# A graph kernel's first layer: gathers that wait for edge counts, and counts put ahead of a group's sums

## The chip, the cores and the metric

The kernel runs on one core of one Trainium2 chip. The metric is the device time of one execution in microseconds. Engines are named as the profile has them: PE is TensorE's matrix multiply (PEld its weight loads), DVE is VectorE, ACT is ScalarE, POOL is GpSimd, SP is SyncE.

## The reference

Four graph layers over 6,250 nodes of 128 features and 206,250 edges, each followed by a residual sum and a layer norm:

```python
x = _layernorm(x + _L0_gnn_ref(x, ..., src, dst, edge_type_8), axis=-1)   # two relational layers
x = _layernorm(x + _L1_gnn_ref(x, src, dst), axis=-1)                     # sum over neighbours
x = _layernorm(x + _L2_gnn_ref(x, edge_index, ...), axis=-1)              # attention over 12,500 slots
x = _layernorm(x + _L3_gnn_ref(x, edge_attr_128, src, dst), axis=-1)      # sum of node and edge rows
```

The first relational layer, which is where the change lies, is per node

```python
T = jnp.einsum('nd,rdf->rnf', h, W)
msg = T[etype, src] * norm
agg = jax.ops.segment_sum(msg, dst, num_segments=N)
h = relu(bn(agg + h @ self_loop[l]))
```

Edges are sorted by their target `dst`.

## The kernel before

The program runs through phases: preparation, first layer (`phase_first`), second relational layer, the neighbour sum, attention, the edge sum. The later phases work on dense matrices of edge counts (how many edges go from node a to node b), and the first layer makes these counts beside its own work.

**A tile of the first layer.** 6,250 nodes are 49 tiles of 128 targets (`NT`). The edges of a tile lie in 35 slots of 128 edges (`SLOTS`), in 7 groups of 5 (`GROUPS`, `PER`). For each group:

- SyncE waits on `ring` until the same group of the tile before is summed, then loads the edges' records (L627) and their attribute rows (L631).
- GpSimd waits for the records (`rec_in`), then issues 5 indirect DMAs, one per slot, each of which gathers 128 rows of the table of messages into `rows` (L643). When they have landed, `gathered[g]` has risen.
- VectorE makes 0/1 masks of the edges' targets (`hot`, L1024, and `rows`' last columns, L1025) and raises `hot_made`.
- TensorE waits for `gathered`, `hot_made` and `attr_in`, and adds the group into one PSUM bank by 5 matmuls, mask by rows (L756; a 4-byte matmul shows as two records, so a group is x10). The last one raises `ring`.

After group 6 VectorE takes the sum out (`take`, L948) and `close` makes the node's new row.

**The counts.** TensorE also ranks the edges of a tile by source tile (`rank_quarter` in groups 0 to 3, L662 and L665; `rank_left` in group 4, L672 and L677), VectorE turns ranks into places, and TensorE places the edges (`place`, L688, in group 0 of the next tile). For the tile t - 1, during the groups of tile t, TensorE makes the counts by small matmuls of 32 rows (`count`, L700 and L705). The 49 source tiles are 4 blocks (`BLOCKS`) of 16, 16, 16 and 1. Blocks 0 to 3 are done in groups 2 to 5, each after that group's sum and ranking. A block is 8 + 64 matmuls (8 + 4 for the last), all four quarters into the one PSUM tensor `cnt`.

**What orders the counts.** `count(t, b)` waits for VectorE's `shot` masks (`shot_made`, L1008) and for `cnt_moved`, that is until ScalarE has copied all of block b - 1 out of `cnt` (L857, four copies) into `mine`. TensorE turns the copied counts by transposes (`turn_counts`, L723): turn 0 in group 3, 1 in group 4, 2 in group 5, 3 in group 6 (`FLIP_AT`), turns 4 to 6 of the tile before that in groups 0 to 2 (`FLIP_LATER`), always as the last work of the group. ScalarE works strictly in its program's order: for block b it first does `move_turned(t, b - 1)`, which waits for turn b - 1, makes two copies (L816, L817) and issues two stores (L821), and only then waits for `counted` and copies block b out. For block 0 it is `move_turned(t - 1, 6)` that stands ahead.

`counted` starts at 2 and rises by one for each block; `ring` starts at 7. Both are counted up over all tiles. The order of each engine's work is written out by hand in the blocks of `phase_first`; no planner orders it.

Of the kernel before, what the change touches and what calls it, by code (L numbers as in the profile page):

```python
# [19 lines left out]
NT = -(-NODES // P)  # L20
# [27 lines left out]
BLOCKS = [(b * BANK, min(BANK, NT - b * BANK)) for b in range(-(-NT // BANK))]  # L48
# [474 lines left out]
    return r  # L523


def phase_first(nc, k):

    with ExitStack() as ctx:
# [3 lines left out]
        def sem(name):  # L532
            k.sems.append(nc.alloc_semaphore(name="f_" + name))
            return k.sems[-1]
# [72 lines left out]
        srow_out, shot_made, counted, cnt_moved, stored = sem("srow_out"), sem("shot_made"), sem("counted"), sem("cnt_moved"), sem("stored")  # L607
# [6 lines left out]
        @block.sync  # L614
        def _(e):
            with e.Fori(0, NT) as t:
                for u in range(QUARTERS):
                    c = e.value_load(k.wlo[0:1, bass.ds(t * QUARTERS + u, 1)], min_val=0, max_val=REAL_CHUNKS)
                    e.wait_ge(wrec_used, t)
                    e.dma_start(wrec[:, u * QCOLS:(u + 1) * QCOLS, :].rearrange("p a b -> p (a b)"),  # L620
                                k.rec_d[bass.ds(c * (CHUNK * REC), P * QCOLS * REC)].rearrange("(p c) -> p c", p=P))\
                     .then_inc(wrec_in, 16)
                c = e.value_load(k.tlo[0:1, bass.ds(t, 1)], min_val=0, max_val=REAL_CHUNKS)
                for g in range(GROUPS):
                    s = slice(g * PER, (g + 1) * PER)
                    e.wait_ge(ring, t * GROUPS + (g + 1))
                    e.dma_start(recs[:, s, :].rearrange("p a b -> p (a b)"),  # L627
                                k.rec_d[bass.ds(c * (CHUNK * REC), P * SLOTS * REC)]
                                .rearrange("(p c) -> p c", p=P)[:, g * PER * REC:(g + 1) * PER * REC])\
                     .then_inc(rec_in[g], 16)  # L630
                    e.dma_start(rows[:, s, D:2 * D],  # L631
                                k.ins["edge_attr_128"][bass.ds(c * CHUNK, P * SLOTS), :]
                                .rearrange("(p j) f -> p j f", p=P)[:, s, :]).then_inc(attr_in[g], 16)

        @block.gpsimd
        def _(e):
            with e.Fori(0, NT) as t:
                for g in range(GROUPS):
                    e.wait_ge(rec_in[g], (t + 1) * 16)
                    e.wait_ge(ring, t * GROUPS + (g + 1))  # L640
                    e.sem_inc(turn, 1)
                    for j in range(g * PER, (g + 1) * PER):
                        e.indirect_dma_start(  # L643
                            out=rows[:, j, 0:D], out_offset=None, in_=k.table_d[0],
                            in_offset=bass.IndirectOffsetOnAxis(ap=recs[:, j, 4:5].bitcast(I32), axis=0),
                        ).then_inc(gathered[g], 16)

        @block.tensor
        def _(e):
# [30 lines left out]
            def place(t, first):  # L680

                e.wait_ge(puts_made, t + 1)
                if not first:
                    e.wait_ge(by_dst_moved, t * NSEG - (NSEG - GROUPS + len(FLIP_LATER)))
                for u in range(QUARTERS):
                    for c in range(QCOLS):
                        a = u * QCOLS + c
                        m = e.matmul(pm[0:CELLS + 1, u * 3 * QW:(u + 1) * 3 * QW], put_col[:, a, :],  # L688
                                     put_row[:, a, :, :].rearrange("p x r -> p (x r)"), start=c == 0, stop=c == QCOLS - 1)
                m.then_inc(placed, 1)  # L690

            def count(t, b):

                lo, n = BLOCKS[b]
                e.wait_ge(shot_made, t * (len(BLOCKS) + 1) + (b + 2))
                e.wait_ge(cnt_moved, (t * len(BLOCKS) + b) * QUARTERS)
                for i in range(2):
                    for u in range(QUARTERS):
                        q = slice(u * QW, (u + 1) * QW)
                        e.matmul(cnt[:, u, 0:n * QW], shotx[q, i, :], xhot[q, i, lo * QW:(lo + n) * QW],  # L700
                                 start=i == 0, stop=False)
                for j in range(n):
                    for u in range(QUARTERS):
                        q = slice(u * QW, (u + 1) * QW)
                        m = e.matmul(cnt[:, u, j * QW:(j + 1) * QW], shot[q, b % 2, j, :], dhot[q, lo + j, :],  # L705
                                     start=False, stop=j == n - 1)
                m.then_inc(counted, 1)
# [18 lines left out]
            def turn_keys(t):  # L726

                e.wait_ge(key_moved, t + 1)
                for x in range(3):
                    m = e.transpose(kk[:, x, :], key_t[:, x, :], k.ident16[:, :])  # L730
                m.then_inc(key_ps, 1)
# [16 lines left out]
            def tile(t, first, second):  # L748
                for g in range(GROUPS):
                    e.wait_ge(gathered[g], (t + 1) * (16 * PER))  # L750
                    e.wait_ge(hot_made, t * GROUPS + (g + 1))
                    e.wait_ge(attr_in[g], (t + 1) * 16)
                    if g == 0:
                        e.wait_ge(acc_free, t)
                    for j in range(g * PER, (g + 1) * PER):
                        m = e.matmul(acc[:, 0:GW], hot[:, j, :], rows[:, j, :], start=j == 0, stop=j == SLOTS - 1)  # L756
                    m.then_inc(ring, 1)
                    if g == 0 and not first:
                        place(t - 1, second)
                    if g < QUARTERS:  # L760
                        rank_quarter(t, g)
                    if g == QUARTERS:
                        rank_left(t)
                    if not first:
                        if g == 0:
                            turn_keys(t - 1)
                        if g == 1:
                            turn_h(t - 1, second)
                        if g == 2:
                            self_terms(t - 1, second)  # L770
                        if 2 <= g < 2 + len(BLOCKS):
                            count(t - 1, g - 2)
                        if g in FLIP_AT:
                            turn_counts(t - 1, FLIP_AT[g])
                        elif not second:
                            turn_counts(t - 2, FLIP_LATER[g])
# [1524 lines left out]
```

## Time and profile before

| | us |
|---|---|
| median of 3 runs | 6612.25 |
| lowest, highest | 6593.21, 6656.78 |
| profiled execution, own time | 6709.38 |
| its span | 6707.6 |

The profile is that of one execution. Its page gives busy times and shares of each engine, waits with their releasers (an arrow `<-` names who ended the wait; "issue" is a wait for nothing that the profile shows; "remote" one whose releaser it cannot name), and the timeline gives single instructions in order of time, merged where they follow each other. A row of the windows view has the stretch, its length, then busy us and instructions of PE, PEld, DVE, ACT and POOL, the granted clock of TensorE, the DMA engines' busy share and GB/s. The DMA queue q0 is GpSimd's. In a timeline row the first number is the start and the second the length, both in us.

### The profile page before, as it was taken

The numbers are of one execution on the slowest core, as the hardware profiler recorded it, in microseconds if no ns is written. First come the engines' busy times: TensorE is split into PE (matmuls) and PEld (weight loads), VectorE is DVE, ScalarE is ACT, GpSimd is POOL, SyncE is SP. The second block draws the span as 40 slices with busy tenths as digits, with TensorE's granted clock in tenths as the row PEclk, the third lists the DMA queues.
The fourth block names the chain that finished last, engine by engine and source line by source line (L and its number), as shares of the span: only waits on it lengthen the run. The fifth ranks groups of instructions, "written<-read, shape, count | busy, mean of one in ns | idle before, by whom it ended". The sixth has DMA issues, their size and how long they took to land. (4 is left out here: it accounts for less than half of the span.)

```text
span 6707.6 us, 157901 instructions
## 1 busy us (share of the span) xinstructions
PE 4545.6 (68%) x54120; PEld 3396.8 (51%) x54121; DVE 3830.7 (57%) x8330; ACT 2425.1 (36%) x3822; POOL 2436.6 (36%) x2046
## 2 busy tenths in 40 slices
PE   5465655656555555555655499999989466666778
PEld 2244444444444444444444366666645266666767
DVE  4155555554455544545545566666630689999843
ACT  2123333233233223223223366666610145555600
POOL 0444544444444444444444000000000067777700
PEclk8677777777777777777777699999989778888889
DMA  5444444444444444444444422222258234444378
GB/s 201 132 123 138 146 142 136 134 138 138 134 135 137 133 127 137 134 129 142 138 128 146 137 77 77 80 77 76 80 193 284 74 148 153 153 153 153 105 249 259
DMA packets 673171, 935.65 MB, mean 139 GB/s; under 512 B 150771, under 2 KB 567006, under 8 KB 666174
## 3 DMA queue, kind: packets, MB, share of 16 engines
q1 hardware_dynamic: 470114, 548.86, 25.7%
q10 hardware_dynamic: 146524, 270.11, 10.9%
q0 software_dynamic: 56448, 115.72, 6.9%
q8 instruction: 32, 0.52, 0.0%
q14 instruction: 53, 0.43, 0.0%
HBM read 653.23 MB, written 281.17 MB: 139 GB/s over the span
## 5 line engine op out<-in xcount | busy, mean ns | idle before, releaser
L643 POOL DMA_INDIRECT f_rows<-table,f_recs x1715 | 1652.8, 964 | 1960.1 <-DMA f_recs<-edge_records 1162.4
L756 PE MATMUL f_acc<-f_rows,f_hot 128*128 128x264 f32 x3430 | 1181.9, 509 | 368.3 <-issue 295.4
L756 PEld LDWEIGHTS f_acc<-f_rows,f_hot 128*128 128x128 f32 x3430 | 848.5, 257 | 567.2 <-issue 351.9
L2013 PE MATMUL a_psum<-state_and_spare,a_weights 128*128 (+1 forms) x4802 | 662.4, 308 | 296.9 <-DVE a_weights L2131 152.4
L1963 POOL TENSOR_TENSOR a_weights<-a_powers,a_counts 128x896 f32<-128x896 f16 x245 | 719.6, 2945 | 336.9 <-ACT a_powers L2053 305.9
L2013 PEld LDWEIGHTS a_psum<-state_and_spare,a_weights 128*128 128x128 f32 x4802 | 651.6, 224 | 310.6 <-issue 203.8
L1224 ACT ACTIVATE g_grow<-g_gps 128x512 f16<-128x512 f32 x1225 | 667.1, 595 | 343.1 <-PE g_gps L1161 342.6
L816 ACT ACTIVATE f_counts_by_destination<-f_pm 128x896 f16<-128x896 f16 x343 | 314.7, 917 | 1085.3 <-PE f_pm L723 864.2
L705 PE MATMUL f_cnt<-f_dhot,state_and_spare 32*128 32x32 f16 x9604 | 238.4, 182 | 643.2 <-issue 642.7
L1181 PE MATMUL g_zps<-g_ohot,g_grow 32*128 32x256 f16 x19992 | 655.3, 269 | 0.7 <-issue 0.6
L1263 DVE TENSOR_SCALAR g_ohot<-count,slot_target 128x256 f16<-128x256 f16 x2499 | 537.1, 281 | 153.1 <-PE g_zps L1181 147.8
L1008 DVE TENSOR_TENSOR state_and_spare<-f_count_up,f_key 128x2048 f16<-128x2048 f16 x196 | 349.6, 1784 | 419.8 <-PE f_cnt L705 347.7
L897 DVE TENSOR_TENSOR f_put_row<-f_sort,f_by_cell 128x490 f16<-128x490 f32 x196 | 130.4, 665 | 740.1 <-PE f_sort L665 413.8
L705 PEld LDWEIGHTS f_cnt<-f_dhot,state_and_spare 32*128 32x128 f16 x9604 | 170.1, 95 | 746.3 <-issue 715.8
L1181 PEld LDWEIGHTS g_zps<-g_ohot,g_grow 32*128 32x128 f16 x19992 | 457.9, 93 | 158.5 <-issue 119.4
L1145 POOL DMA_INDIRECT g_grow<-high_low_rows,g_lcur x49 | 46.4, 946 | 1142.1 <-PE g_zps L1181 1142.1
L2117 DVE SCALAR_TENSOR_TENSOR a_powers<-a_psum,a_leaky_from,a_diag 128x896 f32 (+1 forms) x343 | 379.0, 1141 | 59.7 <-POOL a_weights L1963 37.7
L857 ACT ACTIVATE state_and_spare<-f_cnt 128x512 f16<-128x512 f32 (+1 forms) x784 | 326.4, 502 | 225.7 <-issue 223.9
L1161 PE MATMUL g_gps<-g_hl,g_shot 128*128 128x256 f16 (+1 forms) x2450 | 378.2, 275 | 35.1 <-DVE g_shot L1254 35.1
L2088 DVE CUSTOM_DVE_ANT_0 a_pen<-self_term,a_pen 128x6272 bf16<-128x6272 f32 x49 | 372.2, 7596 | 2.5 <-issue 1.1
L2051 ACT ACTIVATE a_powers<-a_powers,a_leaky_from x245 | 252.8, 1032 | 281.4 <-DVE a_powers L2117 279.2
L817 ACT ACTIVATE f_pen<-f_pm,f_far 128x896 bf16<-128x896 f16 x343 | 343.7, 1002 | 0.0
(272 smaller groups left out, 5923.7 us busy)
## 6 DMA issues: line engine op xcount, KB each, us to landing
f_rows<-in_edge_attr SPq DMA_DIRECT2D x343, 320.0 KB
g_srow<-slot_sources SPq DMA_DIRECT2D x245, 320.0 KB
counts_by_destination_f<-f_counts_by_destination ACTq DMA_DIRECT2D x343, 224.0 KB
no_edge_penalty<-f_pen ACTq DMA_DIRECT2D x343, 224.0 KB
s_ring<-counts_by_destination_f SPq DMA_DIRECT2D x98, 784.0 KB
a_pen<-no_edge_penalty SPq DMA_DIRECT2D x49, 1568.0 KB, 9.9
a_counts<-counts_by_source_f SPq DMA_DIRECT2D x49, 1568.0 KB, 6.7
e_ring<-counts_by_source_f SPq DMA_DIRECT2D x343, 224.0 KB, 3.8
```

What stands on the lines that cost most here:

```text
L643: e.indirect_dma_start(out=rows[:, j, 0:D], out_offset=None, in_=k.table_d[0], in_offset=bass.IndirectOffsetOnAxis(ap=recs[:, j, 4:5].bitc ...
L705: m = e.matmul(cnt[:, u, j * QW:(j + 1) * QW], shot[q, b % 2, j, :], dhot[q, lo + j, :], start=False, stop=j == n - 1)
L756: m = e.matmul(acc[:, 0:GW], hot[:, j, :], rows[:, j, :], start=j == 0, stop=j == SLOTS - 1)
L1008: e.tensor_tensor(shot[:, b % 2, 0:n, :], repeat(count_up[:, 0:P], n), spread(key[:, 1, lo:lo + n], P), ALU.is_equal).then_inc(shot_made, 1)
L1161: m = e.matmul(gps[:, h % GBANKS, c % 2 * 2 * D:(c % 2 + 1) * 2 * D], shot[:, c // SPIECE, c % SPIECE * P:(c % SPIECE + 1) * P], rows, sta ...
L1181: m = e.matmul(zps[:, u, 0:RELATIONS * QW], grow[s, gslot(b), i, q * D:(q + 1) * D], ohot[s, oslot(b), i, :], start=c == 0 and q == 0, sto ...
L1224: e.activation(grow[:, gslot(b), PAIRS[h][0] % BATCH:(PAIRS[h][1] - 1) % BATCH + 1, :], gps[:, h % GBANKS, :].rearrange("p (i f) -> p i f" ...
L1263: m = e.tensor_scalar(ohot[:, oslot(b), i, :], k.count16[:, 0:RELATIONS * QW], k.key_r[:, bass.ds(t, 1), c:c + 1].rearrange("p a c -> p (a ...
L1963: e.tensor_tensor(weights[:, j, :].rearrange("p (i c) -> p i c", c=P), powers[:, bass.ds(n & 3, 1), :].rearrange("p a (i c) -> p (a i) c", ...
L2013: m = e.matmul(psum[:, 4 + i // 3, i % 3 * (D + 4):i % 3 * (D + 4) + D + 1], weights[:, j, i * P:(i + 1) * P], k.msg[:, bass.ds(hb * SEG + ...
L2088: e.tensor_tensor_reduce(out=pen[:, w, :], in0=frow, in1=pen[:, w, :], scale=1.0, scalar=FAR, op0=ALU.subtract, op1=ALU.max, accum_out=bes ...
L2117: e.scalar_tensor_tensor(powers[:, bass.ds(n & 3, 1), :].rearrange("p a c -> p (a c)"), bank2(0)[:, 0:SW], leaky_from[:, 2, b:b + 1], leak ...
```

## The change

In `phase_first` alone. On TensorE, `count(t - 1, b)` is called in the same group as before (2 to 5), but after the group's three waits and ahead of its sum, not after sum, ranking and self term. On GpSimd, the gathers of groups 3 to 6 get one more wait each, from the second tile on: until `counted` has reached (t - 1) * 4 + g, which is when `count(t - 1, g - 3)` is done, the block that TensorE counts in group g - 1. For this the first tile is taken out of GpSimd's loop.

```diff
+COUNT_AT = 2
...
         @block.gpsimd
         def _(e):
-            with e.Fori(0, NT) as t:
+            def tile(t, first):
                 for g in range(GROUPS):
                     e.wait_ge(rec_in[g], (t + 1) * 16)
                     e.wait_ge(ring, t * GROUPS + (g + 1))
+                    if COUNT_AT < g <= COUNT_AT + len(BLOCKS) and not first:
+                        e.wait_ge(counted, (t - 1) * len(BLOCKS) + (g - COUNT_AT + 2))
                     e.sem_inc(turn, 1)
...
+            tile(0, True)
+            with e.Fori(1, NT) as t:
+                tile(t, False)
...
                     e.wait_ge(attr_in[g], (t + 1) * 16)
+                    if COUNT_AT <= g < COUNT_AT + len(BLOCKS) and not first:
+                        count(t - 1, g - COUNT_AT)
                     if g == 0:
                         e.wait_ge(acc_free, t)
...
                             self_terms(t - 1, second)
-                        if 2 <= g < 2 + len(BLOCKS):
-                            count(t - 1, g - 2)
                         if g in FLIP_AT:
```

## Rows read from the trace of the kernel before

**Rows 1.** Page, head and part 1: busy us, share of the span, instructions

```profile
span 6707.6 us, 157901 instructions
...
PE 4545.6 (68%) x54120; PEld 3396.8 (51%) x54121; DVE 3830.7 (57%) x8330; ACT 2425.1 (36%) x3822; POOL 2436.6 (36%) x2046
```

**Rows 2.** Windows (busy us, instructions), then line L948: starts of closings

```profile
226.00:3742.00 3516.00, 2064.05 (x21363) 1510.58 (x21363) 1791.56 (x3547) 1015.08 (x1716) 1652.80 (x1715) 0.77 0.44 134
...
L948 DVE COPY f_agg<-f_acc x49: 431/433/434, 311.9 to 3741.4; 128x264 f32<-128x264 f32 x49
```

**Rows 3.** Timeline of PE: start us, length us, what, [idle before <- releaser]

```profile
1946.73 2.44 PE L756 MATMUL f_acc<-f_rows,f_hot 128*128 128x264 f32 x10
...
1972.96 4.04 PE L756 MATMUL f_acc<-f_rows,f_hot 128*128 128x264 f32 x10 [2.66 <-issue]
...
1978.03 0.47 PE L746 MATMUL f_pm<-loop_weights,f_ht 128*128 128x128 f32 x2
1978.43 0.61 PE L700 MATMUL f_cnt<-f_xhot,f_shotx 32*128 32x512 f16 x8
...
1989.49 0.56 PE L705 MATMUL f_cnt<-f_dhot,state_and_spare 32*128 32x32 f16 x41 [1.22 <-issue]
1990.04 0.91 PE L723 MATMUL f_pm<-ident,state_and_spare 128*128 128x128 f16 x7
...
1996.15 0.61 PE L700 MATMUL f_cnt<-f_xhot,f_shotx 32*128 32x512 f16 x8 [0.56 <-ACT state_and_spare L857]
...
1997.26 0.55 PE L723 MATMUL f_pm<-ident,state_and_spare 128*128 128x128 f16 x7
...
2009.46 1.04 PE L700 MATMUL f_cnt<-f_xhot,f_shotx 32*128 32x512 f16 x8 [3.02 <-ACT state_and_spare L857]
...
2014.67 0.93 PE L723 MATMUL f_pm<-ident,state_and_spare 128*128 128x128 f16 x7
...
2020.72 0.22 PE L700 MATMUL f_cnt<-f_xhot,f_shotx 32*128 32x32 f16 x8 [0.62 <-ACT state_and_spare L857]
...
2021.36 2.44 PE L756 MATMUL f_acc<-f_rows,f_hot 128*128 128x264 f32 x10
```

**Rows 4.** Timeline of DVE, the masks for the third sum

```profile
1971.99 0.81 DVE L1024 TENSOR_TENSOR f_hot<-f_count_up,f_recs 128x640 f32<-128x640 f32 x1
```

**Rows 5.** Timeline of POOL: first and last of 15 calls, two later ones

```profile
1968.21 0.94 POOL L643 DMA_INDIRECT f_rows<-table,f_recs  x1 [7.79 <-PE f_acc L756]
...
1985.70 0.94 POOL L643 DMA_INDIRECT f_rows<-table,f_recs  x1 [0.30 <-issue]
1997.19 0.94 POOL L643 DMA_INDIRECT f_rows<-table,f_recs  x1 [10.55 <-DMA f_recs<-edge_records]
...
2012.18 0.95 POOL L643 DMA_INDIRECT f_rows<-table,f_recs  x1 [0.30 <-issue]
```

**Rows 6.** Waits in 400 to 3700 us: sum us, times, longest

```profile
PE f_cnt L705 <- issue: 634.3, 683, 2.6
```

**Rows 7.** Timeline of ACT: transposes taken up, counts copied out

```profile
2004.44 0.92 ACT L816 ACTIVATE f_counts_by_destination<-f_pm 128x896 f16<-128x896 f16 x1 [8.35 <-remote]
...
2015.63 0.92 ACT L816 ACTIVATE f_counts_by_destination<-f_pm 128x896 f16<-128x896 f16 x1 [6.23 <-PE f_pm L723]
...
2018.60 2.06 ACT L857 ACTIVATE state_and_spare<-f_cnt 128x512 f16<-128x512 f32 x4 [1.15 <-issue]
```

**Rows 8.** Timelines of POOL and PE in the first tile

```profile
232.03 0.95 POOL L643 DMA_INDIRECT f_rows<-table,f_recs  x1 [0.30 <-issue]
...
236.86 4.76 PE L756 MATMUL f_acc<-f_rows,f_hot 128*128 128x264 f32 x10 [20.94 <-DMA f_rows<-table,f_recs]
...
299.69 5.80 PE L756 MATMUL f_acc<-f_rows,f_hot 128*128 128x264 f32 x16
```

**Rows 9.** DMA in 2013.8 to 2014.5 us, then in 2014.5 to 2016.5: packets

```profile
q0 software_dynamic: 32, 0.07, 36.6%
...
DMA packets 0, 0.00 MB, mean 0 GB/s; under 512 B 0, under 2 KB 0, under 8 KB 0
```

## Prediction

> **What bounds the kernel now.** I read the page's busy shares first [rows 1]: the profiled execution has a span of 6707.6 us (6709.4 by its own time), and no engine is over 68% busy, so the shares say only that waits decide. The edit touches one stage alone, so the next view is the stretch and the line that closes a tile [rows 2]: the first layer fills 226 to 3742 us, GpSimd works in 1652.8 of these 3516 us, and the 49 closings run from 311.9 to 3741.4, so a tile takes (3741.4 - 311.9)/48 = 71.4 us. All that follows is the price of one tile, times 48 (the first tile is not changed).
>
> Then one tile in order of time, from the end of one tile's last sum (1946.73 + 2.44 = 1949.17) to the next (2021.36 + 2.44 = 2023.80), 74.6 us [rows 3]. The reader is to see four things in it:
>
> - The third sum starts at 1972.96, right after VectorE's masks for it (1971.99) [rows 3, 4], 23.8 us into the tile.
> - The counts of block 0 run from 1978.43 to 1990.04, 11.6 us; the same 72 matmuls for block 1 run from 1996.15 to 1997.26, 1.1 us; block 2 takes 2009.46 to 2014.67, 5.2 us [rows 3]. GpSimd issues gathers without a break from 1968.21 to 1986.64, starts again at 1997.19, and issues the next ones up to 2013.13 [rows 5]. The slow blocks are those that stand beside gathers, the fast one had none beside it. The waits table gives the sum: TensorE stood idle inside the counts for 634.3 us in 400 to 3700 us, 683 times [rows 6], or 634.3/3300 x 71.4 = 13.7 us per tile.
> - A second thing stretches beside gathers: signals of TensorE. The transposes that end at 1997.81 are taken up by ScalarE at 2004.44, 6.6 us late, with gathers issued from 1997.19 on; those that end at 2015.60, with no gather being issued, are taken up at 2015.63 [rows 3, 5, 7].
> - Between two blocks ScalarE is the link: transposes done at 2015.60, two copies, two DMA issues, then four copies out of the count bank at 2018.60, and the next block starts at 2020.72 [rows 3, 7]: 5.1 us from the end of the transposes to the next counts.
>
> So the path through a tile is VectorE's masks, then counts, transposes, ScalarE, three times over, with sums hidden in ScalarE's 5.1 us. The gathers themselves are a tile ahead; nobody waits for them after the first tile.
>
> **The change, part by part.** It adds no arithmetic. It adds 4 waits per tile on GpSimd and moves 4 counts ahead of 4 sums. A gather of group g, 3 to 6, now waits for the counts that TensorE does in group g - 1 of the *same* tile, where it had been issued a tile earlier. Behind it on GpSimd's queue stand all later gathers, groups 0 to 2 of the next tile included. Per tile:
>
> *Gains.* All four counts now run while GpSimd is held, so 13.7 us of idle time go, and of the late signals those that followed a count (6.6 us in this tile). The first counts start when the third sum did, 23.8 us into the tile, rather than after it.
>
> *Losses.* (a) The transposes that free ScalarE for the next block still stand at the end of their group, now behind the sum and the ranking of that group. These were hidden in ScalarE's 5.1 us, and now they come before it. (b) The last group's gather starts only after the last counts, so its issue and its landing come onto the path. A group is five calls; fifteen of them start between 1968.21 and 1985.70 [rows 5], one each 1.25 us, and the last takes 0.94: 5.95 us from first start to last end. (c) The gathers of groups 6, 0, 1, 2 become one run of 20 calls, 25 us, in which the tile's last signal falls.
>
> The new tile, added up from its start:
>
> 1. Start to first counts: 23.8 us as now [rows 3, 4]. The closing signal of a tile now lies 11 us deep in the run of calls. Bounds for its delay: 0 (the 0.03 us of [rows 7]), and the first tile, where the last sum ends at 299.69 + 5.80 = 305.49 and VectorE takes the sum at 311.9 [rows 2, 8], 6.4 us. I take 2, nearer to the low end, since in that first tile the run before had lasted longer. 25.8 us.
> 2. Counts of block 0: 1.1 us.
> 3. Sum, ranking, self term, transposes: 1972.96 to 1978.50 is 5.5, transposes 0.6, then ScalarE's 5.1 [rows 3, 7]; delay of the signal between 0.03 and 6.6 us; I take 1.2, since the gather of this group ends by the time the transposes do and then delays nothing. 12.4 us.
> 4. Counts of block 1: 1.1. Sum, ranking, transposes 5.6, delay 1.2, ScalarE 5.1: 11.9.
> 5. Counts of block 2: 1.1. Sum, the short ranking, transposes 4.8, delay 1.2, ScalarE 5.1: 11.1.
> 6. Counts of block 3: 0.25 (1 of the 49 tiles of columns).
> 7. Gather of group 6: 0.3 to start, 5.95 to issue, then landing. With calls that end at 2013.13, the queue's last 32 packets ran between 2013.8 and 2014.5 and it had none afterwards [rows 9], so 0.7 to 1.4 us; in the crowded first tile the sum began at 236.86, 3.9 us after the calls' end at 232.98 [rows 8]. I take 1.7, nearest to the steady rows. Then the last sum, 2.44 at the full clock [rows 3], 4.76 at half [rows 8]; TensorE has just idled some 3 us, I take 3.6. Together 11.6 us. The sum and transposes of group 5 hide in it.
>
> Sum: 25.8 + 1.1 + 12.4 + 1.1 + 11.9 + 1.1 + 11.1 + 0.25 + 11.6 = 76.4 us, against 71.4: 5.0 us more, x 48 = 240 us. ScalarE's path between two counts (11.1 to 12.4) stays longer than the gather's (0.3 + 5.95 + 1.7 = 8.0), so in the middle of the tile the gathers stay hidden; that cover ends when a landing takes over 4.8 us. The sum is made against the profiled execution's 6709.4 us; the median of the runs is 6612.25, 97 us (1.4%) less, and I put the same 240 us on it.
>
> The full clock is 2.4 GHz, half is 1.2 GHz. Each ScalarE wait of 5.1 us is idle time of TensorE ahead of the next sum, and sums that follow idle time run slow (4.76 us [rows 8], 4.04 after 2.7 us of idle time [rows 3]), so steps 3 to 5 hold a mixed price of about 3.7 us for a sum.
>
> *A rule that speaks against the change.* The Trainium skill, "SBUF — State Buffer", section "SBUF: two separate sides", holds that DMA traffic cannot slow an engine and that TensorE never waits for another engine at the memory; only VectorE and GpSimd share a port. By it the gathers would not be what stretches the counts, nothing would be gained by parting them, and the time would be that of the last rival below. The trace differs (11.6 us against 1.1 us for one piece of work), though it does not say what is shared.
>
> **Rivals.**
>
> *Signals on time and a warm TensorE (faster).* Same chain, delays 0, all sums at 2.44: 23.8 + 1.1 + 10.0 + 1.1 + 9.5 + 1.1 + 8.6 + 0.25 + 9.9 = 65.4 us, 6.0 less per tile, -290 us at most. It decides once delays and slow sums together cost 5 us less than I charge; a midway 68 us gives 6612 - 165 = 6450. For it: each run of gathers between counts is only 5 calls long, and the late signals of now are mostly beside counts. Against it: idle stretches of 5 us in every group, and the run of 20 calls.
>
> *Gains and losses cancel.* Delays 0 with my sums: 76.4 - 2 - 3.6 = 70.8 us, -30 us: 6580 to 6680.
>
> *The gathers become the bound.* If they land 3.9 us late, as in the first tile, step 7 costs 2.2 us more, and a late signal of 6.4 at the tile's end 4.4 more: 83 us, +560, about 7170. Against it: the steady landing of 1.4 us.
>
> *The counts stay slow whatever GpSimd does* (their stretch has another cause, such as the signals of ScalarE's stores). Then 13.7 us stay: 90 us per tile, +900, about 7500. Against it: block 1's 1.1 us in the same tile.
>
> **How the numbers follow.** Chances: my sum 0.48, cancelled 0.15, faster rival 0.17, gathers bind 0.15, counts stay slow 0.05. The prediction is 6612 + 240, rounded to 6850 us. The range reaches to the edge of the cancelled case and a bit into the faster one below, 6560, and above past the middle between my sum and the gathers' case, 7040 (9 us per tile more than now). About 1% is what a measurement of this kernel can tell from no change: faster 0.17, same 0.15, slower 0.68.
>
> **What would show it right or wrong.** In the changed kernel's trace: (1) the four counts of a tile take 1.1 us or little over, and idle time inside them is gone; (2) between two counts there are 11 to 12.5 us, and ScalarE's copies out of the count bank end it; (3) GpSimd shows single runs of 5 calls in the middle of a tile and one of 20 across its end, each ended wait of a middle run being on TensorE's counts; (4) the last sum of a tile waits for the gather; (5) the closings lie 76 us apart. The prediction is wrong if signals arrive within 0.1 us beside gathers (then the tile is near 70 us), if the sums run at 2.44 us throughout, or if a group's gather is what the counts wait for.

## The result, and the profile after

| | before, same chip | after |
|---|---|---|
| median, us | 6619.99 (4 runs) | 7313.61 (4 runs) |
| lowest, highest | 6593.21, 6656.78 | 7306.9, 7323.04 |
| ratio, 95% interval | | 1.1014, 1.0979 to 1.1049 |
| span of the profiled execution | 6707.6 | 7321.3 |

The kernel became slower by 694 us, where I had forecast 240. The direction and the place held, the size did not: it lies outside the range.

Head, windows and closings of the changed kernel; these answer to [rows 1, 2]:

```profile
span 7321.3 us, 158083 instructions
...
226.00:3742.00 3516.00, 1839.74 (x18094) 1366.75 (x18095) 1512.47 (x3007) 856.30 (x1450) 1374.50 (x1456) 0.72 0.37 114
...
L957 DVE COPY f_agg<-f_acc x49: 432/433/434, 307.6 to 4369.7; 128x264 f32<-128x264 f32 x49
```

The closings lie (4369.7 - 307.6)/48 = 84.63 us apart, where [rows 2] gave 71.45. All engines do less in the same 3516 us, and the granted clock of TensorE is 0.72 where it was 0.77: it waits more, and its sums run slower. 13.2 us a tile, x 48, is 633 us, where the two profiled spans differ by 614, so all of the loss stands in the first layer.

One tile on PE, from the end of a last sum (2254.76) to the next (2336.36). Compare with [rows 3]:

```profile
2254.57 0.58 PE L732 MATMUL f_pm<-ident,state_and_spare 128*128 128x128 f16 x7
2259.93 4.74 PE L767 MATMUL f_acc<-f_rows,f_hot 128*128 128x264 f32 x10 [4.78 <-issue]
2268.08 3.26 PE L697 MATMUL f_pm<-f_put_row,state_and_spare 128*52 128x96 f16 x40 [3.41 <-issue]
...
2281.56 0.73 PE L709 MATMUL f_cnt<-f_xhot,f_shotx 32*128 32x512 f16 x8 [2.70 <-DVE f_rows L1034]
2282.06 0.73 PE L714 MATMUL f_cnt<-f_dhot,state_and_spare 32*128 32x32 f16 x64
2282.72 3.77 PE L767 MATMUL f_acc<-f_rows,f_hot 128*128 128x264 f32 x10
...
2288.53 0.55 PE L732 MATMUL f_pm<-ident,state_and_spare 128*128 128x128 f16 x7 [0.55 <-issue]
2295.85 1.04 PE L709 MATMUL f_cnt<-f_xhot,f_shotx 32*128 32x512 f16 x8 [6.76 <-ACT state_and_spare L866]
2296.68 0.72 PE L714 MATMUL f_cnt<-f_dhot,state_and_spare 32*128 32x32 f16 x64
...
2301.65 0.55 PE L732 MATMUL f_pm<-ident,state_and_spare 128*128 128x128 f16 x7
2307.57 1.04 PE L709 MATMUL f_cnt<-f_xhot,f_shotx 32*128 32x512 f16 x8 [5.36 <-ACT state_and_spare L866]
...
2313.39 0.55 PE L732 MATMUL f_pm<-ident,state_and_spare 128*128 128x128 f16 x7
2322.07 0.24 PE L709 MATMUL f_cnt<-f_xhot,f_shotx 32*128 32x32 f16 x8 [8.12 <-ACT state_and_spare L866]
...
2331.62 4.74 PE L767 MATMUL f_acc<-f_rows,f_hot 128*128 128x264 f32 x10 [4.50 <-DMA f_rows<-table,f_recs]
```

The counts themselves are free of stalls, as forecast: block 0 takes 1.23 us, where [rows 3] had 11.6. The last sum waits for its gather, as forecast. The new thing is near the top: `place` (L697) starts only 3.41 us after sum 0 has ended, and takes 3.26 us. Behind it on its engine stand sum 1, the first counts and sum 2.

What GpSimd does meanwhile (the second row is the last call of a run of 20), and when ScalarE takes up the transposes (L732) that ended at 2255.15, 2289.08, 2302.20 and 2313.94:

```profile
2254.00 0.94 POOL L648 DMA_INDIRECT f_rows<-table,f_recs  x1 [0.30 <-issue]
...
2265.23 0.94 POOL L648 DMA_INDIRECT f_rows<-table,f_recs  x1 [0.30 <-issue]
2283.64 0.94 POOL L648 DMA_INDIRECT f_rows<-table,f_recs  x1 [17.46 <-PE f_cnt L714]
...
2298.24 0.94 POOL L648 DMA_INDIRECT f_rows<-table,f_recs  x1 [8.68 <-PE f_cnt L714]
...
2309.96 0.94 POOL L648 DMA_INDIRECT f_rows<-table,f_recs  x1 [5.78 <-PE f_cnt L714]
...
2323.16 0.94 POOL L648 DMA_INDIRECT f_rows<-table,f_recs  x1 [7.26 <-PE f_cnt L714]
```
```profile
2266.19 0.92 ACT L825 ACTIVATE f_counts_by_destination<-f_pm 128x896 f16<-128x896 f16 x1 [17.38 <-remote]
...
2290.68 0.92 ACT L825 ACTIVATE f_counts_by_destination<-f_pm 128x896 f16<-128x896 f16 x1 [2.29 <-remote]
2302.54 0.92 ACT L825 ACTIVATE f_counts_by_destination<-f_pm 128x896 f16<-128x896 f16 x1 [6.75 <-PE f_pm L732]
2316.98 0.92 ACT L825 ACTIVATE f_counts_by_destination<-f_pm 128x896 f16<-128x896 f16 x1 [9.47 <-remote]
```

The transposes of group 6 (done at 2255.15) are taken up at 2266.19, 11.0 us late, with the end of the run of 20 calls (2265.23 + 0.94 = 2266.17). Those of group 4 (2313.94) are 3.0 us late. Averaged over the tiles the first are 12.9 us late. It is the signal that comes late, and not ScalarE that is slow to see it: the trace also holds the times at which semaphores were raised, which no view prints, and there the one for these transposes is raised at 2266.08, 0.11 us before ScalarE starts (0.11 too in the 42 tiles with a delay of over 3 us for which the trace has that time). TensorE itself had begun its next sum at 2259.93. The signal of the tile's sum, 0.4 us earlier, was on time for VectorE: the sum ends at 2254.76, and the closing's row, of DVE, is

```profile
2254.89 0.43 DVE L957 COPY f_agg<-f_acc 128x264 f32<-128x264 f32 x1 [17.23 <-PE f_acc L767]
```

The sum was taken within 0.15 us in most tiles, over 0.5 us late in 9 of the 49, and never over 3.2. The waits table in 400 to 4300 us has the same two things in sum, GpSimd held by counts and ScalarE by transposes:

```profile
POOL f_rows L648 <- PE f_cnt L714: 1949.7, 184, 21.2
ACT f_counts_by_destination L825 <- remote: 1415.5, 119, 20.9
```

### The profile page after: what moved, and what is told of

It is laid out like the page before. It is cut to its first block and busy times, and to the rows that moved or that the text cites. A ratio compares the mean times of both kernels' runs of the same rounds, so it can differ in the third digit from the quotient of the medians.

```text
span 7321.3 us, 158083 instructions
## 1 busy us (share of the span) xinstructions
PE 4642.6 (63%) x54120; PEld 3490.2 (48%) x54121; DVE 3815.6 (52%) x8330; ACT 2425.0 (33%) x3822; POOL 2414.6 (33%) x2046
## 5 line engine op out<-in xcount | busy, mean ns | idle before, releaser
L648 POOL DMA_INDIRECT f_rows<-table,f_recs x1715 | 1619.4, 944 | 2659.0 <-PE f_cnt L714 2046.1
L767 PE MATMUL f_acc<-f_rows,f_hot 128*128 128x264 f32 x3430 | 1355.4, 568 | 480.3 <-DMA f_rows<-table,f_recs 236.4
L767 PEld LDWEIGHTS f_acc<-f_rows,f_hot 128*128 128x128 f32 x3430 | 958.8, 291 | 730.0 <-issue 470.0
L709 PE MATMUL f_cnt<-f_xhot,f_shotx 32*128 32x512 f16 (+1 forms) x1568 | 149.0, 465 | 1123.4 <-ACT state_and_spare L866 991.8
L709 PEld LDWEIGHTS f_cnt<-f_xhot,f_shotx 32*128 32x128 f16 x1568 | 26.4, 102 | 1156.9 <-ACT state_and_spare L866 986.7
L957 DVE COPY f_agg<-f_acc 128x264 f32<-128x264 f32 x49 | 21.2, 433 | 841.4 <-PE f_acc L767 770.4
```

The source lines that it names most:

```text
L648: e.indirect_dma_start(out=rows[:, j, 0:D], out_offset=None, in_=k.table_d[0], in_offset=bass.IndirectOffsetOnAxis(ap=recs[:, j, 4:5].bitc ...
```

## The experiments

Each kernel is measured against the kernel before on the same chip. The chips turned out to be of two kinds, and the difference decides how each result is read, so it stands first.

| chip | the kernel before, us | lateness of ScalarE's taking up transposes, at the worst place |
|---|---|---|
| of the first comparison | 6619.99 | 12.9 us on average (changed kernel) |
| 8 | 6715.3 | 14.0 us on average (changed kernel) |
| 9 | 6643.51 | up to 6.3 us (kernel before), 7.4 us on average (held a tile ahead) |
| 1 | 5680.84 | 0.13 us |
| 13 | 5692.4 | 0.13 us |

I call 8, 9 and the first "late" chips and 1 and 13 "in-time" ones. All runs of the kernel before within one chip agree within 1% or so. In what follows "tile" is the spacing of the closings over 48 tiles. The kernel before has no trace on an in-time chip. For its tile there I take the 51 us of the kernel that is held a tile ahead (below), which takes the same time.

### Each half of the change alone, and a shorter run at the tile's end (chip 1)

**Order alone.** The changed kernel without GpSimd's new wait:

```diff
-                    if COUNT_AT < g <= COUNT_AT + len(BLOCKS) and not first:
-                        e.wait_ge(counted, (t - 1) * len(BLOCKS) + (g - COUNT_AT + 2))
```

> Counts put ahead of the sums as in the changed kernel, but GpSimd's gathers not held (as before). Theory A (the new order alone costs most: sum and ranking now stand between a block's counts and the transposes that free ScalarE): the gathers still run a tile ahead and still stretch the counts (13.7 us per tile), and about 5.5 us is added between blocks three times, less the 5 us by which the first block starts earlier: some 83 us per tile, about 7150 us. Theory B (the cost is in holding the gathers): the order alone moves little, 71 to 74 us per tile, 6600 to 6750 us.

Measured: 6478.92 us, ratio 1.1407 (1.1304 to 1.151), tile 67.95 us.

**Hold alone.** The changed kernel with `count` back behind the group's sum, ranking and self term:

```diff
-                    if COUNT_AT <= g < COUNT_AT + len(BLOCKS) and not first:
-                        count(t - 1, g - COUNT_AT)
...
+                        if 2 <= g < 2 + len(BLOCKS):
+                            count(t - 1, g - 2)
```

> GpSimd's gathers held as in the changed kernel, counts left behind sum and ranking as before. Both theories: counts run at 1.1 to 1.6 us. Now a group's gather (0.8 to start, 6 to issue, 1.3 to 2 to land) and then its sum (4) and ranking (1.4) stand one behind the other between two blocks, some 14.5 us instead of 12.9 and 10.9: Theory A (gathers held in the same tile are on the path whatever the order): 90 to 96 us per tile, 7500 to 7800 us. Theory B (putting the counts ahead is what hurts): below the changed kernel's 85 us per tile, under 7300 us.

Measured: 7323.65 us, ratio 1.2894 (1.2845 to 1.2943), tile 85.36 us. That lies between the two ranges expected, which had been made from a trace with late signals. It is far above the 71.8 us of the changed kernel on an in-time chip (below): once the gathers are held, putting the counts ahead helps. Sums now wait for gathers, four times a tile, as the waits table in 400 to 3500 us has it:

```profile
PE f_acc L765 <- DMA f_rows<-table,f_recs: 1278.2, 146, 9.3
```

**Shorter run.** The changed kernel, with the gathers of group 1 held until ScalarE has copied out the counts that group 6 transposes, so that the transposes' signal meets no run of calls:

```diff
+                    if g == 1 and not (isinstance(t, int) and t < 2):
+                        e.wait_ge(by_dst_moved, (t - 2) * NSEG + 4)
...
```

> The changed kernel, and the gathers of group 1 also wait until ScalarE has taken over transposes 3 of the tile before, so that the run of 20 calls across a tile's end is parted behind the tenth. Theory A (the signal of these transposes comes 13 us late because of the run, and the placing of edges waits for it): the signal comes within 1 us and the first counts start some 4 us earlier in the tile: 81 us per tile, about 7130 us. Rival (the placing itself, 40 matmuls, is stretched by the calls that now stand beside it): 83.5 to 85 us per tile, 7250 to 7320 us.

Measured: 6678.96 us, ratio 1.1759 (1.1717 to 1.1801), tile 71.81 us. On this chip no signal was late, so this says nothing of lateness, and serves only beside the changed kernel on a like chip (below: 71.75 there, so the shorter run costs and gains nothing when signals come in time).

**Held a tile ahead.** The kernel before, with the gathers of groups 2 to 5 waiting for a count as well, but for one of the tile before, so that they are still issued a tile ahead:

```diff
+                    if held and 2 <= g < 2 + len(BLOCKS):
+                        e.wait_ge(counted, (t - 2) * len(BLOCKS) + (g - 2 + 3))
...
```

> The kernel before with counts in their old place; GpSimd's gathers stay a tile ahead, but those of groups 2 to 5 of the next tile wait for the counts of the same group in this tile. Theory A (counts and signals are stretched by gathers being issued beside them, and that time is real and on the path): the counts take 1.1 to 1.6 us, 5.7 us lie between blocks, and a tile takes 53 to 58 us: 5750 to 5980 us. Rival (the stretch is seen only in the profiled execution, or another wait takes its place): 68 to 72 us per tile, 6450 to 6650 us.

Measured: 5686.04 us, ratio 1.0007 (0.9996 to 1.0018), tile 51.12 us.

What follows: with no late signal at all, either half loses, so the chain of waits alone makes the change slower. Order alone costs 17 us a tile against 51: from one block's counts to the next there are 12.1, 11.0 and 10.4 us, where the kernel that holds a tile ahead has 5.8, 5.9 and 5.6. That is loss (a) of the forecast by itself. Hold alone costs 34 us: nothing of the gather's path has cover when counts stand last in the group. Together they cost 21, less than the 51 of the two added, since counts put in front let the gather go while TensorE does the group's sum. And a hold that keeps the distance of a tile costs nothing here. Neither half alone was run on a late chip.

### The same on a late chip, and the cause of the lateness (chip 8)

**The kernel before, with a profile,** and **the changed kernel**:

> The kernel before, unchanged, for its trace on this chip. On the chip of the four experiments before this one it took 5681 us where the chip of the first comparison took 6620 us. Theory A (the slow counts and late signals beside gathers belong to the first chip or its condition, not to the program): the trace shows counts at 1.1 us and transposes taken up within 0.13 us where the time is near 5680 us, and counts of 10 us where it is near 6620 us. Theory B (the difference lies in another stage): the first layer takes 71 us per tile in both.

> The changed kernel, unchanged. With signals in time its tile adds up as 21.5 us to the first counts and the steps measured with the parted run (1.1, 11.9, 1.5, 11.1, 1.5, 9.7, 0.3, 13.2): 71.8 us per tile, 6680 us, where the kernel before takes 5680 us (ratio 1.18). On a chip with late signals: 85 us per tile, 7310 us (ratio 1.10). Rival (the parting of the run was worth something without late signals too): 75 us per tile, 6840 us.

Measured: 6728.27 us (ratio 1.0019, 0.998 to 1.0058; tile 71.28 us; counts of block 0, 1, 2: 9.96, 2.2, 6.1 us), and 7456.73 us (1.1118, 1.098 to 1.1257; tile 87.77 us; transposes of group 6 late by 14.0 us, those of group 4 by 3.0).

**Transposes in front.** The changed kernel with the transposes of groups 3 to 5 right behind the counts, ahead of the sum. This takes away loss (a):

```diff
                         count(t - 1, g - COUNT_AT)
+                        if 3 <= g <= 5:
+                            turn_counts(t - 1, FLIP_AT[g])
...
-                            turn_counts(t - 1, FLIP_AT[g])
+                            if g == 6:
+                                turn_counts(t - 1, FLIP_AT[g])
```

> The changed kernel with transposes 0, 1 and 2 moved along with the counts, ahead of the group's sum, so that sum and ranking no longer stand between the counts and ScalarE. Theory A (this order is the loss between blocks 1, 2 and 3; what is left is the gather's 8.5 us): 8.8 us instead of 11.1 and 9.7 between these blocks, 3.2 us less per tile: ratio to the kernel before 0.03 below that of the changed kernel (6530 us where that takes 6680). Theory B (the held gathers alone set the steps): no change beyond 1 us per tile.

Measured: 7144.95 us, ratio 1.0653 (1.056 to 1.0746), tile 80.58 us. The links to blocks 2 and 3 fell from 13.1 and 13.0 us to 10.8 each, but not to the 5 that ScalarE needs: the gather is next in line. In the timeline of PE the counts of a block wait, since they stand behind the group's wait on its gather:

```profile
2135.50 1.04 PE L709 MATMUL f_cnt<-f_xhot,f_shotx 32*128 32x512 f16 x8 [5.78 <-DMA f_rows<-table,f_recs]
```

So losses (a) and (b) overlap: this order gives back 7.2 of 16.5 us (87.77 - 71.28), 4.4 of them in the two links and 2.3 ahead of the first counts, where the transposes of group 6 were 8.9 us late instead of 14.0. I had expected 3.2.

**No calls on GpSimd.** The kernel before, with each gather replaced by a plain load of 128 neighbouring rows, issued by SyncE. It leaves out the choice of rows; the bytes are the same:

```diff
+                    for j in range(g * PER, (g + 1) * PER):
+                        e.dma_start(rows[:, j, 0:D], k.table_d[0][bass.ds(t * P, P), :]).then_inc(gathered[g], 16)
...
+            e.wait_ge(ring, GROUPS)
```

> The kernel before with the 35 gathers of a tile replaced by 35 plain loads of 128 table rows each, issued by SyncE: the same bytes in the same piece sizes reach the same tiles, GpSimd does nothing in the first layer. It leaves the choice of rows out, so the sums are those of other rows. Theory A (GpSimd's calls stretch TensorE on the first chip): counts at 1.1 us on any chip, 50 to 55 us per tile, 5650 to 5850 us. Theory B (the DMA traffic does): on a chip where the kernel before takes 6600 us the counts stay at 10 us and the time near 6600. Where the kernel before takes 5680 us both expect 5680.

Measured: 5689.41 us, ratio 0.8483 (0.8411 to 0.8555), tile 51.26 us: on a late chip, the time that the kernel before has on an in-time one.

### Again on an in-time chip, with the changed kernel itself (chip 13)

Four kernels from above without an edit: held a tile ahead, the changed kernel, order alone, shorter run.

> The kernel with counts in their old place and the gathers of groups 2 to 5 of the next tile held until this group's counts, once more. Where the kernel before takes 5680 us it was equal to it. Where GpSimd's calls stretch TensorE (kernel before at 6600 to 6720 us): its trace without late signals had each of blocks 1 and 2 begin 1.5 us before a run of calls ends, so each would be stretched by some 3.5 us and the rest is free: 58 to 63 us per tile, ratio 0.88 to 0.93. Rival (what is gained at the counts comes back as late signals elsewhere): ratio 0.97 to 1.0.

> The changed kernel beside the others of this call. On a chip with signals in time 71.8 us per tile and ratio 1.18; on one with late signals 85 to 89 us per tile and ratio 1.10 to 1.11.

> Counts in front, gathers not held, once more. It took 68.3 us per tile and ratio 1.14 on the chip with signals in time. Where they are late, the runs of calls meet counts again: 68.3 plus 13.7 us of stretched counts plus late transposes: 82 to 88 us per tile, ratio 1.08 to 1.12. Rival (the counts meet fewer calls in this order): 70 to 75 us, ratio 1.0 to 1.03.

> The changed kernel with group 1's gathers also held until transposes 3 are taken, once more. With signals in time 71.7 us per tile, ratio 1.176. Where they are late: Theory A (the signal of transposes 3, 13 to 14 us late, holds the placing of edges): transposes 3 are taken within 3 us, the first counts start 3 to 4 us earlier than in the changed kernel's 30 us: ratio 0.04 to 0.05 below the changed kernel's in this call. Rival (the placing is stretched by the calls beside it): equal to the changed kernel within 0.015.

Measured, against 5692.4: 5695.39 us (1.0011, 1.0 to 1.0022; tile 51.16), 6680.24 us (1.1728, 1.1687 to 1.1768; tile 71.75), 6504.11 us (1.1418, 1.1377 to 1.146; tile 67.8) and 6691.35 us (1.1747, 1.17 to 1.1794; tile 71.97). The changed kernel's tile here, on PE and, last row, on ACT, to be held against the one above:

```profile
2003.20 4.49 PE L767 MATMUL f_acc<-f_rows,f_hot 128*128 128x264 f32 x10 [4.77 <-DVE f_rows L1034]
2007.62 1.88 PE L697 MATMUL f_pm<-f_put_row,state_and_spare 128*52 128x96 f16 x40
...
2019.53 0.61 PE L709 MATMUL f_cnt<-f_xhot,f_shotx 32*128 32x512 f16 x8 [2.69 <-DVE f_rows L1034]
...
2050.03 0.55 PE L732 MATMUL f_pm<-ident,state_and_spare 128*128 128x128 f16 x7
2056.37 0.24 PE L709 MATMUL f_cnt<-f_xhot,f_shotx 32*128 32x32 f16 x8 [5.79 <-DMA f_rows<-table,f_recs]
...
2065.94 3.85 PE L767 MATMUL f_acc<-f_rows,f_hot 128*128 128x264 f32 x10 [3.87 <-DMA f_rows<-table,f_recs]
```
```profile
2050.62 0.92 ACT L825 ACTIVATE f_counts_by_destination<-f_pm 128x896 f16<-128x896 f16 x1 [5.47 <-PE f_pm L732]
```

Placing follows sum 0 without a gap and takes 1.88 us instead of 3.26, and the transposes of group 4 (2050.58) are taken up 0.04 us later instead of 3.0. Of that 3.26 no call is the cause, since GpSimd's run had ended at 2266.17: TensorE had idled 3.41 us, and its granted clock was 0.54 in this stretch, where it is 1.00 for the 1.88. Program, work and order are the same; 71.75 us against 84.63 is what late signals cost, with the slower clock behind them.

The counts of block 3 waited here for their group's gather (2056.37) and not for ScalarE, as 42 times in 400 to 3500 us of this trace, once in almost every tile. The forecast had named that as a sign that it is wrong. In the first comparison the signal of group 4 was so late that ScalarE still came last.

### A version that may beat both, and what it is about GpSimd's calls (chip 9)

Held a tile ahead and shorter run, without an edit:

> Gathers a tile ahead, held until the same group's counts. Signals in time: ratio 1.00. Signals late: blocks 1 and 2 begin shortly before a run of calls ends, 58 to 63 us per tile and ratio 0.88 to 0.93; rival (the gain comes back as late signals elsewhere): 0.97 to 1.0.

> The changed kernel with group 1's gathers also held until transposes 3 are taken. Signals in time: ratio 1.175. Signals late: transposes 3 are taken within 3 us and the first counts start 3 to 4 us earlier: ratio 1.05 to 1.07, where the changed kernel had 1.10 to 1.11; rival (the placing is stretched by the calls beside it): 1.10 to 1.11.

**Plain loads from GpSimd.** The kernel before, with each gather replaced by the plain load of above, but issued by GpSimd. It too leaves out the choice of rows:

```diff
-                        e.indirect_dma_start(
-                            out=rows[:, j, 0:D], out_offset=None, in_=k.table_d[0],
...
+                        e.dma_start(rows[:, j, 0:D], k.table_d[0][bass.ds(t * P, P), :]).then_inc(gathered[g], 16)
```

> The kernel before with each indirect gather replaced by a plain load of 128 table rows, still issued by GpSimd at the same places. It leaves the choice of rows out, so the sums are those of other rows. Signals in time: ratio 1.00. Signals late: Theory A (any DMA that GpSimd issues does it): counts still stretched, ratio 0.95 to 1.02; Theory B (only the indirect form does): counts at 1.1 us, ratio 0.85, as with SyncE's loads.

**The kernel before, with a profile:**

> The kernel before, for its trace on this chip: 51 us per tile and counts of 1.1 us where it takes 5690 us, 71 to 73 us per tile and counts of 10 us for block 0 where it takes 6600 to 6720 us.

Measured, against 6643.51: held a tile ahead 6204.4 us, ratio 0.9329 (0.9251 to 0.9408), tile 61.02; shorter run 7203.14, 1.0831 (1.074 to 1.0923), tile 81.99; plain loads 5683.64, 0.8546 (0.8461 to 0.8632), tile 50.92; the kernel before 6641.7, 1.0005 (0.9981 to 1.0028), tile 70.47. The shorter run fell between its two expected ranges.

The matmuls of the counts in 400 to 2600 us, by line (busy us, mean ns of one | idle us just before them), for the kernel before on chip 9, no calls on GpSimd on chip 8, and plain loads from GpSimd on chip 9:

```profile
L705 PE MATMUL f_cnt<-f_dhot,state_and_spare 32*128 32x32 f16 x6076 | 155.4, 182 | 416.4 <-issue 416.0
```
```profile
L698 PE MATMUL f_cnt<-f_dhot,state_and_spare 32*128 32x32 f16 x8300 | 92.0, 176 | 0.0
```
```profile
L702 PE MATMUL f_cnt<-f_dhot,state_and_spare 32*128 32x32 f16 x8492 | 93.9, 176 | 0.0
```

The same line for the kernel held a tile ahead, first on chip 1 and then on chip 9:

```profile
L712 PE MATMUL f_cnt<-f_dhot,state_and_spare 32*128 32x32 f16 x8428 | 94.3, 176 | 0.1
```
```profile
L712 PE MATMUL f_cnt<-f_dhot,state_and_spare 32*128 32x32 f16 x7056 | 121.5, 181 | 167.6 <-issue 166.7
```

Idle time inside the counts is 416.4 us on the late chip, nothing there when the calls are plain ones, whoever issues them, and nothing on an in-time chip with all indirect calls in place. So it takes both, a late chip and indirect calls under way. Block by block it is the same: in the kernel before on chip 9, the 91 blocks of 72 matmuls (third tile on) that had a call beside them stood idle 6.5 us on average, the other 47 only 0.01; on chip 1, held a tile ahead, 114 blocks had calls beside them and 0.00 us. Traffic is not it: the same bytes per tile flow in the kernels with plain loads, and in less time (190 and 192 GB/s in 400 to 2600 us, where the kernel before has 138). The plain loads differ from the gathers in three things, though. They are not indirect, they fetch rows that lie side by side, and five of them take GpSimd 2.63 us where five indirect ones take 5.94. Which of the three it is stays open.

The hold a tile ahead takes more than half of that idle time away (per tile 167.6/2200 x 61.0 = 4.6 us against 416.4/2200 x 70.5 = 13.3), and no sum waits for its gather, since gathers still come a tile early. It does give something back, at the tile's start, as the rival had it: the transposes of group 6 are taken up 7.4 us late on average, where the kernel before has 1.1 on this chip, and the first counts start 2.4 us later in the tile (30.9 us against 28.5).

In the shorter run the transposes of group 6 are taken up 0.87 us late instead of 12.9, as intended. That gave back 2.6 us of the tile against the changed kernel of the first comparison (81.99 against 84.63; 5.8 against chip 8's 87.77), less than the lateness. These are other chips: the changed kernel was not run on chip 9. Its timeline of PE shows why:

```profile
2118.44 1.99 PE L700 MATMUL f_pm<-f_put_row,state_and_spare 128*52 128x96 f16 x37
2120.94 0.21 PE L700 MATMUL f_pm<-f_put_row,state_and_spare 128*52 128x96 f16 x1 [0.51 <-issue]
2121.65 0.20 PE L700 MATMUL f_pm<-f_put_row,state_and_spare 128*52 128x96 f16 x1 [0.50 <-issue]
2122.37 0.22 PE L700 MATMUL f_pm<-f_put_row,state_and_spare 128*52 128x96 f16 x1 [0.52 <-issue]
```

The five gathers of group 1, moved out of the signal's way, now lie beside placing, which is as dense a stream of small matmuls as the counts are: it took 4.4 us on average (1.9 on an in-time chip), and from the end of sum 0 to sum 1 there were 11.0 us (4.4 in time, 12.1 in the changed kernel). On a late chip the calls must stand somewhere, and a dense stream of small matmuls beside them pays.

## Why the prediction was wrong in size, point by point

Means over the tiles, from the end of one last sum to the next, beside the steps of the forecast; the last column is the changed kernel on chip 13:

| step | forecast | after | in time |
|---|---|---|---|
| 1, start to first counts | 25.8 | 29.6 | 21.5 |
| 2, counts of block 0 | 1.1 | 1.2 | 1.1 |
| 3, to counts of block 1 | 12.4 | 12.9 | 11.9 |
| 4, counts, then to block 2 | 1.1 + 11.9 | 1.55 + 10.9 | 1.55 + 11.1 |
| 5, counts, then to block 3 | 1.1 + 11.1 | 1.55 + 12.9 | 1.55 + 9.7 |
| 6, counts of block 3 | 0.25 | 0.27 | 0.27 |
| 7, gather and last sum | 11.6 | 14.0 | 13.2 |
| sum | 76.4 | 84.9 | 71.8 |

**Step 1 failed, by 3.8 us.** I asked what the run of 20 calls would do to "the tile's last signal" and took the closing sum's, "11 us deep in the run of calls". That one came 0.13 us late in most tiles. The tile's last signal is that of the transposes of group 6, which end 0.4 us after the sum. ScalarE took them up 12.9 us late, twice the 6.4 that I had as my upper bound. It works strictly in order, `place` waits until it has copied them out, and so 12.1 us passed between sum 0 and sum 1 instead of 4.4 in time. I had read in front of me that transposes beside gathers are taken up 6.6 us late [rows 5, 7], and used that number in steps 3 to 5 only; I named nobody as the one waiting for the transposes of group 6. The base was also not clean: my 23.8 us already held some lateness; in time it is 21.5. The new delay is therefore about 8 us, where I charged 2.

**Steps 3 to 5: the mechanism right, one delay too small.** ScalarE ends the wait for the counts, as forecast, and the sum and ranking that once hid behind it now come ahead of it. I charged 1.2 us of lateness to each of the three, as the gather of the group "ends by the time the transposes do". For group 4 the ranking is short, the transposes end 4.0 us into the five calls (2313.94 against 2309.96), and the signal came 3.0 late: step 5 took 1.8 us more than I charged. For group 3, whose transposes are those of step 4, it was 0.8 late, and sum, ranking and transposes took 5.1 us, where I had 5.6: step 4 took 1.0 less. For group 2, in step 3, it was 1.3 late, and step 3 took 0.5 more, 0.3 of it ahead of the signal.

**Counts: 1.55 instead of 1.1 for blocks 1 and 2**, 0.9 us together. I had their length from a tile where the sum stood ahead of them [rows 3]. Now idle time does, the first 8 matmuls take 1.04 instead of 0.61 us, and the granted clock over the stretch fell from 0.77 to 0.72.

**Step 7, 2.4 us too little.** GpSimd started 0.84 us after the counts, not 0.3. Issuing took 5.94, as charged. From there to the sum 2.56 us passed, where I charged 1.7 from the queue's last packet; a packet's end is not yet the sum's start. The sum took 4.7 us, the value at 1.2 GHz, where I had put 3.6 between the two levels.

Together 3.8 + 0.1 + 0.5 - 0.6 + 2.3 + 2.4 = 8.5 us, x 48 = 408 of the 464 us that the forecast was short. The rest comes from moving a difference of profiled executions to medians: the one before lies 89 us above its median, the one after 9, which makes 80 us. Against it stand some 20 us by which the rest of the span was shorter after.

**What held.** The points (1), (3) and (4) that I named for the trace are there: counts free of stalls, runs of 5 and of 20 calls that wait for counts, a last sum that waits for its gather. (2), 11 to 12.5 us between counts, held to within half a microsecond. (5), 76 us, did not.

**The rivals.** Of "gains and losses cancel" (70.8 us, delays 0 with my sums) the tile was measured as it stood: 71.75 us on chip 13. But nothing cancels there, as on that chip the kernel before needs 51 and has no stall to gain. Of "the gathers become the bound", the price (83 us, 7170) was nearest, and for half of its reason: the late signal at the tile's end was it, slower landing was little of it (0.9 us more than I charged, where that rival had 2.2). "The counts stay slow" fell: blocks 0 to 2 took 1.55 us at most in every tile. With it I had weighed a rule of the Trainium skill, "SBUF — State Buffer", section "SBUF: two separate sides", that DMA traffic and engines do not slow each other. Chips 1 and 13 behave by it (0.1 us idle in 8428 matmuls), and the bytes were not the cause on the others either; yet there TensorE's small matmuls did stall beside GpSimd's indirect calls (416.4 us), and its signals did come late.

**The gain of 13.7 us** that I set against the losses is real on late chips: 9.96, 2.2 and 6.1 us became 1.35, 1.55 and 1.55 on chip 8. It was spent by the two waits that the change itself put on the path (some 21 us: 71.75 against 51.16 on chip 13) and by the lateness moved to group 6's transposes.

## What to carry to other kernels

When a producer must keep out of the way of some work, hold it against that work of an earlier step, so that its lead stays: the same idea with the distance of a tile kept gave 0.93 on a late chip and 1.00 on an in-time one, where the change gave 1.10 and 1.17. Before work is put in front, look for what it had been hiding behind another engine, here the sums behind ScalarE's 5 us. And when a busy stretch of one engine is made longer, list every signal that will fall into it, and for each who waits for it; the one that matters may be the one 0.4 us after the one looked at.

## What the runs showed of the hardware that I had not expected

- **The same program takes 5681 to 5692 us on two chips and 6620 to 6715 us on three.** Nearly all of the difference lies in the first layer: (71.45 - 51.12) x 48 = 976 us of the 1022 between the spans of the first comparison's kernel before and of the one held a tile ahead on chip 1. What is seen there is TensorE's dense small matmuls stretched beside GpSimd's indirect DMA calls (13.7 of these 20.3 us a tile are idle time inside the counts, by the sum made from [rows 6]), and its signals coming late. A trace from one chip shows only that chip's behaviour: I argued from 11.6 against 1.1 us for the same work as if it were general, and the "before" of my sum, 71.4 us a tile, is 51 elsewhere. What differs between the chips is open.
- **Not every signal in a run of calls is late.** The transposes of group 5 end some 4 us into the run of 20 and were 0.04 us late; those of group 4 end 4 us into a run of 5 and were 3.0 late; those of group 6, on average 13.7 us into the run with 11.0 left, were 12.9 late. That is 2 us after the run's end on average, but with a spread from 4 us before it to 3.6 after, so the end of the run is not shown to be what releases them. What tells them apart was not tried.
- **Plain loads leave no trace of this on a late chip.** 0.0 us idle inside the counts, 5684 us in all from GpSimd and 5689 from SyncE, the level of an in-time chip.
